# A fused transformer block: both value halves of the second batch element ahead of the transposes of the first one's probabilities

## The reference

```python
def reference(x, ctx_1024, ...):
    x = x + xattn(layernorm(x), ctx_1024, ctx_1024, Wq, bq, Wk, bk, Wv, bv, Wo, bo)
    x = x + attn(layernorm(x), w_qkv, b_qkv, w_out, b_out)
    x = x + ffn(layernorm(x), w_gate, w_up, w_down)
    return x

def xattn(queries, keys, values, ...):      # 16 heads of 16
    q = (queries @ Wq.T + bq).reshape(B, L, H, E)
    k = (keys @ Wk.T + bk).reshape(B, S, H, E)
    v = (values @ Wv.T + bv).reshape(B, S, H, E)
    scores = jnp.einsum('blhe,bshe->bhls', q, k)
    attn = jax.nn.softmax(scores * E ** -0.5, axis=-1)
    out = jnp.einsum('bhls,bshe->blhe', attn, v).reshape(B, L, H * E)
    return out @ Wo.T + bo
```

## Time and profile before

| what | value |
|---|---|
| median of 3 runs | 925.13 us (923.7 to 926.21) |
| the profiled execution | 928.29 us, of which the span of its instructions is 926.5 us |
| mean granted TensorE clock | 0.988 |
| PE busy | 95% of the span |
| DVE busy | 82% |
| ACT busy | 75% |
| POOL busy | 47% |

### The profile page before, as it was taken

One profiled execution on the slowest core, in us unless ns is written; L12 is line 12 of the kernel. 1 busy time (PEld: TensorE's weight loads), 2 busy tenths in 40 slices (PEclk: granted clock), 3 DMA queues, 4 the chain that ended last, 5 costly groups with the idle time before them and its releaser, 6 DMA issues. The chain is left out here.

```text
span 926.5 us, 28280 instructions
## 1 busy us (share of the span) xinstructions
PE 881.8 (95%) x9650; PEld 738.5 (80%) x9666; DVE 757.8 (82%) x1587; ACT 697.1 (75%) x2046; POOL 431.6 (47%) x643
## 2 busy tenths in 40 slices
PE   6999999999999999999999988999999996899997
PEld 5888988888888988988898877878877874566664
DVE  5878778888888888877887776988888885999996
ACT  4777887777777777787777665777777774899996
POOL 3333333333333343334333327676767651677775
PEclk9999999999999999999999989999999997999999
DMA  6222111111111101111111000000000000000101
GB/s 180 94 90 78 40 45 31 40 47 40 33 41 40 45 28 40 45 40 38 36 40 40 23 2 1 2 1 0 1 0 0 1 2 2 20 32 29 34 29 40
DMA packets 31637, 31.86 MB, mean 34 GB/s; under 512 B 3280, under 2 KB 30800, under 8 KB 31568
## 3 DMA queue, kind: packets, MB, share of 16 engines
q1 hardware_dynamic: 30448, 30.47, 10.6%
q10 hardware_dynamic: 1120, 0.59, 0.2%
HBM read 26.86 MB, written 4.19 MB: 34 GB/s over the span
## 5 line engine op out<-in xcount | busy, mean ns | idle before, releaser
L503 ACT ACTIVATE probs<-psum,nmax 128x256 f32<-128x256 f32 x512 | 237.8, 488 | 63.5 <-DVE nmax L460 62.7
L460 DVE TENSOR_REDUCE nmax<-psum 128x2 f32<-128x512 f32 x256 | 159.0, 684 | 24.1 <-PE psum L329 23.4
L342 PE MATMUL psum<-id_sb,probs 128*128 128x128 f32 x1024 | 125.8, 275 | 0.6 <-ACT probs L503 0.5
L511 POOL TENSOR_TENSOR rstd<-vare,minus_half 128x1 f32<-128x1 f32 x96 | 53.1, 553 | 154.5 <-DVE vare L398 152.0
L527 POOL TENSOR_TENSOR cl<-c_sb,ch 128x512 fp32r<-128x512 f32 x64 | 81.6, 1275 | 78.8 <-ACT ch L478 78.8
L342 PEld LDWEIGHTS psum<-id_sb,probs 128*128 128x128 f32 x1024 | 113.9, 141 | 3.6 <-ACT probs L503 3.0
L484 ACT ACTIVATE probsT<-psum 128x512 f32<-128x512 f32 x160 | 89.5, 603 | 32.0 <-PE psum L342 31.8
L503 ACT ACTIVATION_READ_ACCUMULATOR probs<-psum,nmax 128x1 f32 x512 | 112.6, 220 | 0.0
L534 POOL TENSOR_TENSOR rm<-rinv,hm_sb 128x256 f32<-128x256 f32 x64 | 39.7, 621 | 120.8 <-DVE rinv L437 120.8
L329 PE MATMUL psum<-k_sb,qb 32*128 32x256 f32 x1024 | 88.6, 400 | 3.8 <-DVE k_sb L413 1.8
L329 PEld LDWEIGHTS psum<-k_sb,qb 32*128 32x128 f32 x1024 | 62.0, 184 | 15.4 <-issue 10.8
(11 more groups left out here) (139 smaller groups left out, 2334.3 us busy)
## 6 DMA issues: line engine op xcount, KB each, us to landing
c_sb<-in_ctx_t SPq DMA_DIRECT2D x64, 256.0 KB, 2.7
x_sb<-in_x SPq DMA_DIRECT2D x32, 128.0 KB, 2.4
out<-y_sb SPq DMA_DIRECT2D x32, 128.0 KB, 1.7
w_all<-in_w_gate SPq DMA_DIRECT2D x1, 1024.0 KB, 5.1
w_all<-in_w_up SPq DMA_DIRECT2D x1, 1024.0 KB, 5.1
w_all<-in_w_down SPq DMA_DIRECT2D x1, 1024.0 KB, 5.9
wqkv_sb<-in_w_qkv SPq DMA_DIRECT2D x1, 768.0 KB, 4.8
wk_sb<-in_wk ACTq DMA_DIRECT2D x1, 256.0 KB, 3.9
```

Source lines behind the costliest of these rows:

```text
L342: last = nc.tensor.transpose(sp[g][:, c:c + P], probs[:, 2 * g + u, kh * P:(kh + 1) * P], id_sb[:])
L460: nc.vector.tensor_reduce(nmax[:, 2 * g:2 * g + 2], sp[g].rearrange("p (u s) -> p u s", u=2), AX.X, ALU.max, negate=True).then_inc(max_don ...
L503: nc.scalar.activation(probs[:, j, :], sp[g][:, u * S:(u + 1) * S], ACT.Exp, bias=nmax[:, j:j + 1], accum_out=rsum[:, j:j + 1]).then_inc(e ...
```

## The change

In the bodies of the cross-attention the second value half of (t, 1) moves from behind the output projection to the place right behind the first half, ahead of the transposes of (t, 0). The loop's body and the written-out last tile change alike. The other place at which the value halves are split, in the second half step, stays as it is. No other engine's program changes.

```diff
                 def body(t, n, j, first=False, wsum=False, ahead2=True):

                     pe_k(pe, t, 1)
-                    pe_v(pe, t, 1, (0,))
+                    pe_v(pe, t, 1)
                     pe_transpose(pe, t, 0)
                     if not first:
                         pe_out(pe, t - 1)
-                    pe_v(pe, t, 1, (1,))
                     if ahead2:
                         pe_xt(pe, t + 2, xt_ps)
                     pe_scores(pe, t, 1, n, j)
...
                 t = NT - 1
                 pe_k(pe, t, 1)
-                pe_v(pe, t, 1, (0,))
+                pe_v(pe, t, 1)
                 pe_transpose(pe, t, 0)
                 pe_out(pe, t - 1)
-                pe_v(pe, t, 1, (1,))
                 pe.wait_ge(k_ev, 2 * NT)
                 pe_xt2(pe, 0, x0_ps)
```

## The result

The changed kernel takes 946.07 us in the median of 4 runs (945.29 to 947.0), against 925.67 us for the kernel before in its 4 runs. The ratio is 1.0217, with a 95% interval from 1.0197 to 1.0237: 20.4 us slower, where 19.8 was forecast. The profiled execution took 946.49 us, with a span of 944.7 us.

The account below looks back on a forecast made before the run. The prediction took the chain OUT, y, XT to set each body's pace. OUT later by 31 x 0.71 - 2.2 = 19.8 us, with nothing gained behind it, gave 925.1 + 19.8 = 944.9 us; 8-in-10 range 937 to 949.

Parts of the forecast that it names:

- The chain OUT, y, XT: Cross-attention bodies: XT waits for y, not the value half, because of their shared half bank; 1.64 us after OUT, 1.75 in loops.
- T later by 0.71 us, less the wait that comes back: Six matmuls ahead of T delay it in 31 bodies; 2.2 us waiting for exponentials return, so OUT is 19.8 us later.
- Nothing gained behind OUT: Removing six matmuls between OUT and XT was costed at nothing, at most 4 us over all; PE idles there instead.
- No second wait appears: S reaches group 2's bank 1.24 us after y's start, its copy ends at 1.02 us, so S meets no added wait.
- The gaps further on: Rival, 10%: PE's gaps in the second half step, before K and S, take up 9.3 us of the shift; 935.6 us.
- No effect: Rival, 5%: XT is not held by y, the six matmuls only change places on PE; 925.1 us.
- Faster: Rival, 3%: PE's own list paces S, so waits inside T and ahead of XT get filled; 919.4 us.
- the rival on the clock: Rival, 4%: the new PE hole between OUT and XT lowers the granted clock, 0.8 us more per body; 970 us.

Follow-up runs that it names:

- experiment 2: Changed kernel with XT written to the query projection's bank, so that the product with the values waits for y instead of XT: 944.03 us, 1.0200 of the kernel before.
- experiment 7: Kernel before with only VectorE's copy of group 2 moved ahead of y, XT still in the shared half bank: 931.82 us, ratio 1.0077.
- experiment 1: Kernel before with the second value half moved behind XT instead of ahead of T: 942.99 us, ratio 1.0184.
- experiment 8: Kernel before with only XT moved to the query projection's bank, copy of group 2 still behind y: 925.12 us, ratio 0.9997.
- experiment 5: Changed kernel with only VectorE's copy of group 2 moved ahead of y, XT still in the shared half bank: 944.28 us, 1.0207 of the kernel before.
- experiment 9: Changed kernel with XT in the query bank, copy of group 2 ahead of y, and ScalarE's next context split ahead of XT's copies: 923.15 us, 0.9972 of before.
- 3: Changed kernel with XT in the query bank and VectorE's copy of group 2 ahead of y: 916.9 us, 0.9914 of the kernel before.
- 4: Kernel before with XT in the query bank and VectorE's copy of group 2 ahead of y: 916.66 us, ratio 0.9910.
- 6: Kernel before with both value halves moved behind OUT, so that T follows K at once: 939.05 us, ratio 1.0147.

## Why the prediction was right

**The chain OUT, y, XT.** Right, and shown: the profile names y as what XT waits for; cutting the bank's tie brings XT to OUT + 0.86 us (experiment 2); a later y brings a later XT (experiment 7); a hole stays where nothing else is late (experiment 1).

**T later by 0.71 us, less the wait that comes back.** Right. T lasts 1.74 or 1.75 us to OUT in all 31 bodies, and the wait for the exponentials is gone. From the OUT of tile 1 to that of tile 31 it was 542.32 - 38.27 = 504.05 us and is 561.48 - 38.44 = 523.04: 18.99 us over 30 bodies. Two terms were a little large: in the mean of the bodies T starts 1.40 us behind V's first pair instead of 0.70, a shift of 0.70 us and not 0.71, and the excess of T over 1.745 us adds up to 2.05 us over the 31 bodies in the trace of before, not 2.2. Without tile 1's part of 0.16 us, 30 x 0.70 less 1.89 gives 19.1. Two bodies with pieces take 1.38 us more together (33.80 to 35.18, tiles 14 to 16), two in a loop 1.21 (33.54 to 34.75, tiles 24 to 26), as a wait of 0.17 us in every other loop body says.

**Nothing gained behind OUT.** Right: XT is at OUT + 1.64 us, or 1.75 in loops, in all 29 bodies that have one.

**"No second wait appears".** This step was wrong, though the sum didn't depend on it. I took S's 1.31 us for its work and its fourth part for the time at which it reaches group 2. Free of everything S takes 1.07 us, and the copy behind y was a second tie with nearly the same end: OUT + 3.28 us by the copy alone (experiments 2 and 8), 3.24 by the bank alone (experiment 5). Both move with OUT, so the forecast held; but whoever had cut the bank's tie alone on the strength of that paragraph would have found nothing, as experiment 8 shows. The trace of before had a sign of it: between 60 and 560 us its list by lines puts 0.9 us of the idle time ahead of S's weight loads down to DVE's copies to `probsT` (L430).

**The rivals.** The gaps further on did not take the shift up: the pair of bodies grew by 1.38 of the 1.42 us. "No effect" and "Faster" fall with the 20.4 us and with XT at OUT + 1.64 us, where "Faster" asked for less than 0.93. The clock did not fall in the cross-attention: with an idle time of 0.6 to 0.7 us in each body the granted clock is 1.00 over 186 us. The Trainium skill (TensorE: Matmul & The Clock Gate, Part 1) says that the half rate is the default state and that activity releases it; the trace agrees, as PE was busy for 177.56 of these 186 us. The reading of it in the rival on the clock, that each new gap may bring the clock down, is not borne out by gaps of this length. At the start of the next layer the clock falls as before, but less so: the stretch that answers to it, 569.15 to 574.15 us, has 0.72 instead of 0.50. Why it is less is not shown.

```profile
569.15:574.15 5.00, 4.10 (x24) 4.13 (x25) 2.39 (x8) 2.23 (x9) 1.79 (x2) 0.72 0.01 3
```

About 1 us comes back there: the first OUT-like group behind it (line 377, tile 32) moved from 563.13 to 581.20 us, by 18.1, where OUT of tile 31 had moved by 19.2. So the two profiled executions differ by 18.2 us. The medians differ by 20.4, because the profiled execution of the kernel before lies 2.6 us above its median and that of the changed kernel 0.4. Runs of one kernel differ by 2 to 4 us, so that the forecast came within 0.6 us of the measured difference is in part luck; the firmer check is the 18.99 us on PE's timeline.

## What to carry to other kernels

Work that stands behind a producer and ahead of a consumer on an in-order engine may be what hides the round trip through another engine; before moving it, measure the distance from producer to consumer and ask whether it follows the work or the round trip. Two bodies in which the round trip differs by 0.11 us, with the consumer always 0.57 us behind it, were enough to tell. And where two ties end at the same time, cutting either shows nothing (2 us, or a loss) while cutting both is worth 29 us here and 8.5 us on the kernel before, so a null result of one cut is no evidence that the tie is harmless.

## What was unexpected of the hardware

A tensor_scalar on VectorE that reads and writes on-chip memory took 1.54 us instead of 0.48 while a GpSimd subtraction of 1.27 us, started 0.01 us ahead of it, ran (experiment 9). The Trainium skill (SBUF — State Buffer, Who interferes with whom) says that a VectorE instruction in a two-port mode and GpSimd share a pair of ports, that whoever issues first holds it for the whole instruction and the other blocks. The trace agrees in the main: one after the other the two would take 1.27 + 0.48 = 1.75 us, the tensor_scalar ended after 1.54, and the other six, with no such neighbour, keep 0.48. What the missing 0.2 us are, and whether this instruction runs in such a mode, no row shows.

S takes 1.07 or 1.08 us where matmuls run ahead of it (experiments 1, 3, 4 and 6), and 1.25 to 1.29 us straight behind an XT that PE had to wait for (experiments 5 and 7, tile 14), although the copy of group 2 is done early in both. What these 0.2 us are was not tried and stays open.
